# First feed-forward computed by expert in 23 blocks of scattered bf16 rows; second layer entered by halves; third layer's tables loaded earlier

## The chip, the cores and the metric

The kernel is one program on one core of a Trainium2 chip. The metric is the device time of an execution in microseconds, smaller is better. The core's engines are TensorE (PE: matmuls, with PEld its weight loads), VectorE (DVE), ScalarE (ACT), GpSimd (POOL) and SyncE (SP), which here only issues DMAs. The engines run their own instruction streams in order and meet at semaphores. On-chip tensors lie in SBUF; PE writes to eight banks of PSUM, 128 partitions by 512 f32 each.

## The reference

Four layers run over `x` of 2 sequences by 512 tokens by 256 features. Each layer is

```
xn = layernorm(x);  x = x + attention_l(xn) * silu(ffn_l(xn))
```

The change concerns the feed-forward of layer 0, which is computed over all 1024 tokens:

```
shared_out = sigmoid(xn @ shared_gate.T) * (xn @ shared_up.T) @ shared_down.T     # 176 hidden, f32
weights = softmax(xn @ router_w.T)                                                # 8 experts
top_w, top_idx = top_k(weights, 2)
ge, ue = einsum('nh,eih->nei', bf16(xn), bf16(w_gate / w_up))                     # 176 hidden each
de = einsum('nei,ehi->neh', sigmoid(ge) * ue, bf16(w_down))
routed = (bf16(comb)[:, :, None] * de).sum(experts)                               # comb: top_w at top_idx, else 0
return xn + shared_out + routed
```

The layer attention is causal with 16 heads of 16 features in layer 0, plain with 16 query and 4 key heads in layer 1, causal with heads of 128 features in layers 2 and 3. The feed-forward of layer 1 has the same shape as that of layer 0 (8 experts, 2 chosen), but in f32, with silu, a gated shared expert of 352 hidden features and normalised weights.

## The kernel before

Tokens lie in 8 tiles of 128; `B = 2` sequences have `TPB = 4` tiles each. `X` holds the residual, `XN` the normalised rows, `XNT` its transpose, `S` the attention's output. All work is ordered by hand: each engine's program is a list of helpers called layer by layer, and waits on counters between them.

**Start of a layer.** On VectorE `ln_stats` and `ln_scale` each take a half (a sequence); GpSimd computes `rstd` between them (`ln_rstd`). PE turns the rows (`ln_transpose`, L605), ScalarE copies them to `XNT` (`ln_copy`), PE projects (`project01`, L662 and L669 in layer 0, L679 in layer 1). In layer 0 VectorE's `stack_split` makes bf16 parts of queries and keys and PE turns them (L637). In layer 1 GpSimd and VectorE rotate (L488, L489, L1730, L1732), GpSimd computes the RMS factors (L556 to L561), and ScalarE starts the parts with `stack1_first` (L1250). Layer 1 starts after the last row of layer 0's feed-forward; layer 2 is already entered by halves from `shared1`.

**Attention of layers 0 and 1** (`attention01`) runs over `NG = 4` groups of 4 heads and over 8 stages in a group. In layer 0 PE also computes scores for the row maxima of the next group (`max_scores`, L701, L703) in two banks, which VectorE reduces (`row_maxima`, L1765) before PE may write them again. The router's softmax and choice of two experts (`probabilities`, `largest`, L1605 to L1620, and `combine_weights`) run on VectorE in the last group of layer 0.

**Feed-forward of layer 0** (`ffn0`) is dense. In a loop over the two sequences, for 11 tiles of 128 hidden features of all experts, PE computes gate and up (4 bf16 matmuls of 512 columns, L1042) and spreads the combination weights (L1045), ScalarE takes the sigmoid (L1460), and VectorE multiplies twice (L1944, L1947); two tiles of the shared expert are among them. Then for each token tile PE sums 13 matmuls of 256 columns (L1058), and VectorE, ScalarE and VectorE again apply the residual, silu and update (L1961, L1464, L1955, L1957).

**Feed-forward of layer 1.** When its router is done, PE ranks the tokens (`ranks`), VectorE computes a slot for each token and choice (`slots`, 15 operations, L1650 to L1665), and GpSimd scatters the rows of `XN` to `xg` in HBM by 16 indirect DMAs during the attention (`scatter`, in `stage_v`). After the attention, `experts1` runs over `NBLK = 23` blocks of 128 rows, each of one expert. A turn of its loop on PE is

```
turn_rows(i)        # L1073, two transposes
turn_hidden(i - 3)  # L1091, two transposes
owner[i - 1] = pe.value_load(...)   # L1110: the expert's number, from SBUF to a register
gate_up(i - 1)      # L1081, 352 columns, weights' address by the register
down(i - 3)         # L1099, 256 columns, the same
```

with ScalarE at the activation (L1478) and a copy of the turned hidden rows, and VectorE at three operations a block: `store_rows` (L1973), `hidden` (L1979), `store_y` (L1986). SP brings the blocks in fours and writes the results to `yg`. Then PE turns the heads (`turn_heads`, L828) and projects (`out_projection`, L845), while GpSimd gathers each token's two results by 16 more indirect DMAs (`gather`, L524) once the last block is written. `shared1` computes the shared expert (L1132), VectorE multiplies (L2016) and between these sums the gathered rows (`weigh`, L2003, L2004); then come the down matmuls (L1143) and the residual (L2026, L2009, L2010), with the entry of layer 2 in their second half.

**Layer 2's tables.** SP issues `rope2`, `mask_row`, `wa`, `wb` and `bout` after the last down matmul of `shared1` (L401 to L405); VectorE's `attention2` begins with a wait for all five, ahead of its first rotation (L1865).

Of the kernel before, what the change touches and what calls it, by code (L numbers as in the profile page):

```python
# [18 lines left out]
F32 = mybir.dt.float32  # L19
BF16 = mybir.dt.bfloat16  # L20
F16 = mybir.dt.float16
ALU = mybir.AluOpType
# [37 lines left out]
N_CONST = 10  # L60

def build(nc, W, out):
    ctx = ExitStack()
    with ctx:
# [20 lines left out]
        seltab = sb("seltab", [P, E * IE], BF16)  # L86
        sel0 = seltab[0:E, :]
        mask_row = seltab[:, 0:SEQ]
# [13 lines left out]
        combT = sb("combT", [E, TOK], BF16)  # L102
# [63 lines left out]
        NE0 = E * IE  # L166
        w2b = W2[:, :].bitcast(BF16)
        eg0 = w2b[:, 0:DC * NE0].rearrange("p (c n) -> p c n", c=DC)
        eu0 = w2b[:, DC * NE0:2 * DC * NE0].rearrange("p (c n) -> p c n", c=DC)
        ed0 = w2b[:, 2 * DC * NE0:2 * DC * NE0 + 11 * D].rearrange("p (m n) -> p m n", m=11)  # L170
        o = (2 * DC * NE0 + 11 * D) // 2
        sg0 = W2[:, o:o + DC * HS0].rearrange("p (c n) -> p c n", c=DC)
        su0 = W2[:, o + 352:o + 704].rearrange("p (c n) -> p c n", c=DC)
        sd0 = W2[:, o + 704:o + 704 + 2 * D].rearrange("p (m n) -> p m n", m=2)
        I2 = 2 * IE
        HC = IE // 2
        egu1 = W2[:, 0:E * DC * I2].rearrange("p (e c n) -> p e c n", e=E, c=DC)
# [8 lines left out]
        tri_b = W1[:, 800:864].bitcast(BF16)  # L186
        one_b = W1[:, 864:928].bitcast(BF16)
        steps_f = W1[:, 928:992].rearrange("p (e k) -> p e k", e=E)
        upto_f = W1[:, 992:1056].rearrange("p (e k) -> p e k", e=E)
        block_f = W1[:, 1056:1056 + NBLK * E].rearrange("p (n e) -> p n e", e=E)  # L190
# [13 lines left out]
        xb0 = r1b[:, 0:2048].rearrange("p (c t) -> p c t", c=DC)  # L204
        he0 = r1b[:, 2048:2048 + 11 * 512].rearrange("p (m t) -> p m t", m=11)
        hs0 = R1[:, 4096:5120].rearrange("p (m t) -> p m t", m=2)
        act01 = [R1[:, 5120 + 512 * i:5632 + 512 * i] for i in range(2)]
        prod01 = [R1[:, 6144 + 512 * i:6656 + 512 * i] for i in range(2)]
        h1 = R1[:, 7168:7168 + 3 * TOK].rearrange("p (m t) -> p m t", m=3)
        xblk = R2[:, 2048:2048 + 2 * QUAD * D].rearrange("p (r d) -> p r d", d=D)  # L210
        xblkT = [R1[:, 256 * i:256 * i + 256] for i in range(2)]
# [61 lines left out]

        HID0 = [(128 * m, 128) for m in range(11)]
        SH0 = [(0, HS0 // 2), (HS0 // 2, HS0 // 2)]
        SH1 = [(128 * m, min(128, HS1 - 128 * m)) for m in range(3)]

# [1989 lines left out]
```

## Time and profile before

| | us |
|---|---|
| median of 3 runs (lowest, highest) | 1410.25 (1404.46, 1412.22) |
| the profiled execution: its time | 1396.9 |
| its span, first to last instruction | 1395.1 |
| attention of layer 0 ends, heads are turned | 191.4 |
| last row of layer 0's feed-forward | 275.4 |
| layer 1's first `stack1_first` | 296.6 |
| layer 1's blocks | 398.5 to 460.8 |
| layer 2's first rotation | 522.8 |

Positions are from the span's start. PE is busy 90% of the span, so a change moves the time where PE waits, or where PE has less to do and nothing else takes its place. The profiled execution lies 13.3 us below the median of the runs.

### The profile page before, as it was taken

To read this page: it belongs to the slowest core of one execution; us is meant where nothing else is said; L and a number is where in the kernel's file an instruction comes from. 1 tells how busy PE (TensorE), PEld (TensorE's weight loads), DVE (VectorE), ACT (ScalarE), POOL (GpSimd) and SP (SyncE) were. 2 spreads that over 40 slices of the span, in tenths; PEclk is the share of its full clock that TensorE was granted. 3 is DMA by queue.
4 is the path that set the end of the run, shared out by engine and by line. 5 is a ranking of instruction groups with operands and counts; after the bars stand their busy time and mean duration, and the time that the engine had idled before them with its cause. 6 is when DMAs were issued, how large, how long until landed. Compare 5 with 4: busy or idle time off the path is not lost.

```text
span 1395.1 us, 19093 instructions
## 1 busy us (share of the span) xinstructions
PE 1249.1 (90%) x6418; PEld 778.0 (56%) x6418; DVE 743.6 (53%) x2033; ACT 611.6 (44%) x1518; POOL 107.8 (8%) x130
## 2 busy tenths in 40 slices
PE   4888888768999968999999999989999999999994
PEld 3644443344257544556565587656666666666853
DVE  4777625656134258888888740244444434446357
ACT  1634453258952213555555502344444445442053
POOL 3230000052300400000000000000000000000000
PEclk9989999968999988999999999989999999999998
DMA  8000000130212420000000001010000000000000
GB/s 223 12 2 2 2 27 0 54 114 16 77 46 73 147 83 16 12 12 12 13 8 8 5 1 72 9 67 23 12 24 15 20 24 12 24 12 1 1 0 30
DMA packets 25965, 45.75 MB, mean 33 GB/s; under 512 B 3711, under 2 KB 22111, under 8 KB 24551
## 3 DMA queue, kind: packets, MB, share of 16 engines
q1 hardware_dynamic: 23622, 35.25, 7.8%
q0 software_dynamic: 2256, 9.37, 2.3%
q8 instruction: 51, 0.84, 0.2%
q14 instruction: 36, 0.29, 0.1%
HBM read 37.50 MB, written 9.18 MB: 33 GB/s over the span
## 4 chain that ended last, share of the span: by engine, by line
PE 69%; DVE 14%; issue 10%; ACT 4%; DMA 1%; POOL 1%; SPq 1%; ACTq 0%; DVEq 0%; POOLq 0%
PE bank L860 12%; PE bank L876 8%; PE bank L867 8%; PE bank L845 5%; PE bank L853 5%; PE bank L871 4%; PE bank L746 4%; PE bank L730 3%; PE bank L1081 2%; PE bank L1042 2%; DVE W L1765 2%; PE bank L1176 2%; PE bank L1132 1%; PE bank L1099 1%; PE bank L1162 1%
## 5 line engine op out<-in xcount | busy, mean ns | idle before, releaser
L1206 ACT COPY R<-bank 128x512 f32<-128x512 f32 (+4 forms) x203 | 110.5, 560 | 323.4 <-PE bank L876 142.8
L1838 DVE CUSTOM_DVE_ANT_0 bank<-bank,seltab 128x128 f32<-128x128 f32 (+3 forms) x256 | 127.0, 497 | 173.2 <-PE bank L867 170.8
L860 PE MATMUL bank<-XNT,W 128*128 128x512 f32 x416 | 203.3, 613 | 6.8 <-ACT R L1206 3.8
L1343 ACT ACTIVATE R<-bank,nm 128x128 f32<-128x128 f32 (+3 forms) x256 | 136.2, 532 | 109.4 <-DVE nm L1838 108.5
L867 PE MATMUL bank<-R 128*128 128x512 f32 (+3 forms) x384 | 134.3, 434 | 0.0
L860 PEld LDWEIGHTS bank<-XNT,W 128*128 128x128 f32 x416 | 76.4, 194 | 102.8 <-issue 94.7
L1319 ACT ACTIVATE PT<-bank 128x512 f32<-128x512 f32 (+3 forms) x256 | 109.1, 520 | 43.3 <-PE bank L735 40.1
L845 PE MATMUL bank<-W,R 128*128 128x256 f32 x576 | 125.3, 380 | 2.7 <-ACT R L1206 2.7
L845 PEld LDWEIGHTS bank<-W,R 128*128 128x128 f32 x576 | 109.1, 190 | 18.1 <-issue 1.9
L871 PE MATMUL bank<-identf,R 128*128 128x128 f32 x640 | 112.3, 275 | 6.6 <-DVE R L1855 4.9
L876 PE MATMUL bank<-PT,R 128*128 128x128 f32 (+3 forms) x384 | 112.0, 435 | 5.6 <-ACT PT L1206 4.3
L1206 ACT COPY PT<-bank 128x128 f32<-128x128 f32 (+3 forms) x256 | 108.7, 426 | 15.2 <-PE bank L871 15.1
L871 PEld LDWEIGHTS bank<-identf,R 128*128 128x128 f32 x640 | 79.2, 141 | 58.6 <-issue 33.4
L876 PEld LDWEIGHTS bank<-PT,R 128*128 128x128 f32 x384 | 71.2, 190 | 61.4 <-issue 37.8
L853 PEld LDWEIGHTS bank<-W,XNT 128*128 128x128 f32 x640 | 76.5, 192 | 9.5 <-issue 7.6
L853 PE MATMUL bank<-W,XNT 128*128 128x128 f32 x640 | 77.9, 275 | 0.0
L1765 DVE TENSOR_REDUCE W<-bank 128x1 f32<-128x128 f32 (+3 forms) x128 | 57.3, 487 | 26.6 <-PE bank L703 26.6
L730 PE MATMUL bank<-R 96*128 96x512 bf16 (+4 forms) x256 | 66.0, 355 | 5.1 <-DMA R<-W 2.2
L746 PE MATMUL bank<-PT,R 128*32 128x512 f32 (+3 forms) x512 | 59.6, 539 | 0.6 <-ACT PT L1319 0.6
L867 PEld LDWEIGHTS bank<-R 128*128 128x128 f32 x384 | 58.2, 191 | 1.1 <-issue 0.5
L605 PE MATMUL bank<-identf,XN 128*128 128x128 f32 x64 | 15.7, 427 | 44.9 <-DVE XN L1577 44.9
L730 PEld LDWEIGHTS bank<-R 99*128 99x128 bf16 (+1 forms) x256 | 23.1, 100 | 56.3 <-ACT PT L1319 36.3
(258 smaller groups left out, 1819.1 us busy)
## 6 DMA issues: line engine op xcount, KB each, us to landing
W<-in_wq SPq DMA_DIRECT2D x32, 128.0 KB, 2.0
W<-in_wo SPq DMA_DIRECT2D x2, 2048.0 KB, 8.5
W<-in_egu SPq DMA_DIRECT2D x1, 2816.0 KB
W<-in_wk SPq DMA_DIRECT2D x20, 128.0 KB, 2.1
W<-in_wv SPq DMA_DIRECT2D x20, 128.0 KB, 2.0
R<-xg SPq DMA_DIRECT2D x5, 512.0 KB, 4.6
yg<-R SPq DMA_DIRECT2D x5, 512.0 KB, 3.2
W<-in_wa SPq DMA_DIRECT2D x2, 1024.0 KB, 6.4
```

The source lines that it names most:

```text
L730: ins = mm(dst[:, q0:SEQ], kstk[0:rows, g * GH + h if l == 0 else g, b * SEQ + j * P:b * SEQ + (j + 1) * P], qstk[0:rows, g * GH + h, b * ...
L746: ins = mm(PS[OUT_BANK][32 * h:32 * h + 32, q0:SEQ], vs[b][:, j, h if l == 0 else 0, :], PT[:, w % 2, h, q0:SEQ], start=j == 0, stop=j == ...
L845: ins = mm(PS[4 + m % 4][:, 0:D], heads[:, k, m * P:(m + 1) * P], w[:, k, :], start=k == 0, stop=k == n - 1)
L853: ins = mm(bank[:, t * P:(t + 1) * P], XNT[:, c, b * SEQ + t * P:b * SEQ + (t + 1) * P], wqkv23[:, 2, c, :], start=c == 0, stop=c == DC - 1)
L860: ins = mm(bank[:, :], wqkv23[:, s, c, :], XNT[:, c, b * SEQ:(b + 1) * SEQ], start=c == 0, stop=c == DC - 1)
L867: return mm(PS[u % 4][:, 0:n], q[:, t * P:n], k[:, 0:n], start=True, stop=True)
L871: ins = tr(PS[4 + u % 2][:, j * P:(j + 1) * P], Pr[u % 4][:, j * P:(j + 1) * P], identf[:, :])
L876: ins = mm(PS[6][:, j * P:SEQ], v[:, j, :], PT[:, slot, j, j * P:SEQ], start=j == 0, stop=j == TPB - 1)
L1206: return nc.scalar.copy(dst, src)
L1319: fn(PT[:, w % 2, h, q0:SEQ], PS[SCORE_BANK[h]][:, q0:SEQ], ACT.Exp, scale=HD ** -0.5).then_inc(cb["pb_ready"], 1)
L1343: return fn(Pr[c][:, 0:n], PS[c][:, 0:n], ACT.Exp, scale=-1.0, bias=nm[:, c:c + 1], accum_out=esum[:, c:c + 1])
L1838: return dve.tensor_tensor_reduce(out=s[:, 0:n], in0=s[:, 0:n], in1=mask_row[:, SEQ - n:SEQ], scale=-1.0, scalar=-MASKED, op0=ALU.add, op1 ...
```

## The change

Layer 0's feed-forward takes the form of layer 1's. `experts1` and `shared1` become `experts(l)` and `shared(l)`, `ffn0` goes. For layer 0 the rows are cast to bf16 on GpSimd (`xb`) and scattered to an `xg` of their own in groups 2 and 3 of the attention; all matmuls and transposes of its blocks are bf16. The router's work on VectorE moves from the last group into `project01`, the ranks into the start of the attention, the slots into group 1. The routing tables get a place of their own and are loaded at the start, as is `mask_row`. The entry of layer 1 is split by halves, as layer 2's was: the first half is normalised and turned inside `shared(0)`, tiles 0 to 3 are projected, then the second half is turned. Of layer 2's tables, `rope2` and `bout` are issued when layer 1's last gate-up is done, `wa` and `wb` behind the last output projection and ahead of `wo2`. Layer 1's weights are issued after the last residual sum of layer 0.

```diff
@@ SP
-                         (sel0, "sel0"), (rw0, "rw0"),
+                         (mask_row, "mask_row"), (rw0, "rw0"),
+            sp.dma_start(route[:, 0:128].bitcast(BF16), W["route_b"]).then_inc(ld["const"], 16)
+            sp.dma_start(route[:, 128:440], W["route_f"]).then_inc(ld["const"], 16)
...
+            move_blocks(0)
             sp.wait_ge(out_ps, NT)
             sp.dma_start(wqkv1, W["wqkv1"]).then_inc(ld["attn1"], 16)
             sp.dma_start(wo1, W["wo1"]).then_inc(ld["attn1"], 16)
...
-            sp.wait_ge(ffn[0]["y_ps"], NT)
-            sp.wait_ge(zeroed, 32)
+            sp.wait_ge(ffn[0]["f"], NT)
...
+            move_blocks(1)
+            sp.wait_ge(gu_blk, NBLK * 2)
+            sp.dma_start(rope2, W["rope2"]).then_inc(ld["ffn2"], 16)
+            sp.dma_start(bout, W["bout2"]).then_inc(ld["ffn2"], 16)
             sp.wait_ge(out_ps, NT * 2)
-            sp.dma_start(wo23, W["wo2"]).then_inc(ld["wo2"], 16)
-            sp.wait_ge(ffn[1]["y_ps"], NT)
-            sp.dma_start(rope2, W["rope2"]).then_inc(ld["ffn2"], 16)
-            sp.dma_start(mask_row, W["mask_row"]).then_inc(ld["ffn2"], 16)
             sp.dma_start(wa, W["wa2"]).then_inc(ld["ffn2"], 16)
             sp.dma_start(wb, W["wb2"]).then_inc(ld["ffn2"], 16)
-            sp.dma_start(bout, W["bout2"]).then_inc(ld["ffn2"], 16)
+            sp.dma_start(wo23, W["wo2"]).then_inc(ld["wo2"], 16)
@@ GpSimd
+                        if l == 0 and g == 0 and b == 1:
+                            own(pool.tensor_copy(xb, XN[:, :, :]))
+                        scatter(l, SCATTER_AT[l].get(g * B + b, ()))
...
+            pool.dma_start(xg[0].rearrange("(p j) d -> p j d", p=P), zeros_b).then_inc(zeroed, 16)
...
-            pool.wait_ge(coreb[0]["st_ps"], NG * B * GH * TPB)
-            pool.tensor_copy(xb0, XNT[:, :, :]).then_inc(xb_ready, 1)
-            ln_rstd(1)
-            pool.wait_ge(ot_sb, 2)
+            gather(0)
+            pool.wait_ge(ot_sb, LN_PAIRS)
             pool.wait_ge(out_ps, NT)
             pool.memset(R2[:, 0:1024], 1.0).then_inc(const_made, 1)
+            ln_rstd(1)
@@ PE
                 else:
-                    pe.wait_ge(xnt_ready, 2 * LN_PAIRS)
+                    pe.wait_ge(xnt_ready, LN_PAIRS + 2)
                     for m in range(NT):
+                        if m == TPB:
+                            ln_transpose(1, (2, 3))
+                            pe.wait_ge(xnt_ready, 2 * LN_PAIRS)
...
                 if l == 0:
                     stk_copied(0)
                     pe.sem_inc(nm_ps, 2)
+                    ranks(0, PS[0])
...
-                    if l == 1:
-                        experts1()
+                    experts(l)
                     turn_heads(l)
                     out_projection(l, OT01, (wo0, wo1)[l], DC)
-                    if l == 0:
-                        ffn0()
-                    else:
-                        shared1()
+                    shared(l)
@@ ScalarE
-                    for m in range(TPB + 1):
+                    for m in range(TPB):
                         take(m)
+                    ln_copy(1, (2, 3))
+                    take(TPB)
@@ VectorE
                         stack_split(m)
+                        if m == 0:
+                            probabilities(0)
+                        elif m <= 2:
+                            largest(m - 1)
+                        elif m == 3:
+                            chosen(0)
...
-                        if causal and last and w == 0:
-                            probabilities(l)
-                        elif causal and last and w in (1, 2):
-                            largest(w - 1)
-                        elif causal and last and w == 4:
-                            combine_weights()
+                        if causal and g == 1 and w == TPB - 1:
+                            slots()
...
+                    take_ranks(0, PS[0])
...
+                per_gate = NT // (B * nm - 2)
...
+                    if l == 0:
+                        own(stt(out=wx[:, m, :], in0=px[:, 1, m, :], scalar=rs[:, 5, m:m + 1], in1=XN[:, m, :],
+                                op0=ALU.mult, op1=ALU.add))
+                        own(stt(out=wx[:, m, :], in0=px[:, 0, m, :], scalar=rs[:, 4, m:m + 1], in1=wx[:, m, :],
+                                op0=ALU.mult, op1=ALU.add))
...
+                    if 1 <= k < B * nm - 1:
+                        for m in range(per_gate * (k - 1), per_gate * k):
+                            weigh(m)
...
-                ln_stats(2, 1)
+                ln_stats(l + 1, 1)
+                if l == 0:
+                    ln_scale(1, 1)
```

In `shared(0)` the shared expert has two parts of 88 hidden features, so PE's gate-up has 4 steps in place of layer 1's 6 (`nm = 2`), and VectorE weighs tiles 0 to 3 after the second and 4 to 7 after the third (`per_gate = 4`).

## Rows read from the trace of the kernel before

**Rows 1.** The page: engines' totals, and two rows in 40 slices of 34.9 us

```profile
PE 1249.1 (90%) x6418; PEld 778.0 (56%) x6418; DVE 743.6 (53%) x2033; ACT 611.6 (44%) x1518; POOL 107.8 (8%) x130
PEclk9989999968999988999999999989999999999998
```

**Rows 2.** Stretches: length, busy us (x instructions) by engine, granted clock, DMA

```profile
191.40:275.40 84.00, 73.02 (x318) 35.77 (x318) 42.15 (x72) 29.76 (x51) 0.00 (x0) 0.96 0.05 15
275.40:296.60 21.20, 15.89 (x48) 9.91 (x48) 11.73 (x33) 7.95 (x35) 11.43 (x16) 0.76 0.79 259
301.60:325.50 23.90, 15.15 (x133) 14.26 (x134) 18.62 (x50) 15.57 (x31) 13.02 (x23) 0.50 0.00 1
398.50:460.80 62.30, 59.38 (x280) 43.85 (x278) 25.85 (x71) 15.78 (x46) 0.00 (x0) 1.00 0.24 75
```

**Rows 3.** Timeline: PE turns layer 0's heads; ScalarE begins layer 1's parts

```profile
191.44 1.97 PE L828 MATMUL bank<-identf,R 128*128 128x128 f32 x16 [0.81 <-DVE R L1789]
...
296.58 0.93 ACT L1250 ACTIVATE PT<-R,small 128x768 bf16<-128x768 f32 x1 [2.31 <-POOL small L561]
```

**Rows 4.** Groups in 398.5:460.8, layer 1's blocks: busy us, mean ns, idle before

```profile
L1081 PE MATMUL bank<-W,R 128*128 x92 | 31.6, 466 | 1.1 <-DVE R L1973 0.8 <-issue 0.3
...
L1986 DVE COPY R<-bank 128x256 f32<-128x256 f32 x23 | 9.8, 425 | 6.7 <-PE bank L1099 6.7
```

**Rows 5.** PE's sequencer by line, 400.1:401.3 and, last row, 425.8:427.85: duration, first and last start

```profile
L1071 PEldq EVENT_SEMAPHORE  x2: 51/51/51, 400.2 to 401.2; - x2
L1110 PEldq TENSOR_LOAD <-rt x1: 311/311/311, 400.3 to 400.3; - x1
L1081 PEldq FUSED_REGOPS  x2: 46/46/46, 400.9 to 401.1; - x2
...
L1099 PEldq FUSED_REGOPS  x2: 46/53/60, 426.5 to 426.6; - x2
```

**Rows 6.** Timeline, PE: bf16 transposes of layer 0's stack

```profile
37.20 1.99 PE L637 MATMUL bank<-identb,PT 128*96 128x128 bf16 x32 [1.34 <-DVE PT L1685]
```

**Rows 7.** Timeline, layer 1 from its last block to its down matmuls

```profile
460.12 0.42 DVE L1986 COPY R<-bank 128x256 f32<-128x256 f32 x1 [1.48 <-PE bank L1099]
460.80 1.94 PE L828 MATMUL bank<-identf,R 128*128 128x128 f32 x16 [0.72 <-DVE R L1986]
463.87 1.01 POOL L524 DMA_INDIRECT PT<-yg,rt  x1 [80.40 <-DMA yg<-R]
470.58 20.76 PE L1132 MATMUL bank<-XNT,W 128*128 128x512 f32 x48
...
479.38 0.35 DVE L2003 TENSOR_SCALAR PT<-PT,rs 128x256 f32<-128x256 f32 x1 [0.42 <-DMA PT<-yg,rt]
...
482.70 0.95 POOL L524 DMA_INDIRECT PT<-yg,rt  x1 [0.30 <-issue]
...
492.90 8.03 PE L1143 MATMUL bank<-W,R 128*128 128x256 f32 x36 [1.56 <-DVE R L2016]
```

**Rows 8.** Timeline, GpSimd and VectorE at the entries of layers 1 and 2

```profile
288.22 0.83 POOL L488 TENSOR_TENSOR R<-R,rope 128x160 f32<-128x160 f32 x1 [6.82 <-ACT R L1206]
...
294.90 1.64 POOL L561 TENSOR_TENSOR small<-small,mhalf 128x8 f32<-128x8 f32 x1
...
514.76 0.38 DVE L1570 BATCH_NORM_AGGREGATE mv<-stat 128x2 f32<-128x6 f32 x4
...
522.84 0.69 DVE L1865 TENSOR_TENSOR R<-bank,W 128x512 f32<-128x512 f32 x1 [7.70 <-DMA W<-in_bout]
```

**Rows 9.** Timeline, VectorE: in layer 0's projection; layer 1's `slots`, first and last

```profile
43.45 0.69 DVE L1675 TENSOR_TENSOR PT<-bank,PT 128x512 f32<-128x512 f32 x1 [1.17 <-ACT PT L1206]
...
339.27 0.21 DVE L1650 TENSOR_TENSOR rt<-bank,W 128x64 f32<-128x64 f32 x1
...
342.77 0.17 DVE L1665 CAST rt<-W 1x23 int32<-1x23 f32 x1
```

**Rows 10.** Waits in 90:190, layer 0's attention: us in total, times, longest

```profile
PEld bank L701 <- DVE W L1765: 19.5, 39, 1.2
```

More of the change, by code:

```diff
@@ L218, in build, with two @@
-        yg = nc.dram_tensor("yg", (NBLK * P, D), F32, kind="Internal").ap()
+        def two(t, o, n, rows=P):
+            return [t[0:rows, o + n * i:o + n * i + n] for i in range(2)]
+        xb = W2[:, 9216:10240].bitcast(BF16).rearrange("p (m d) -> p m d", m=NT)
+        xblk = (W2[:, 6144:7168].bitcast(BF16).rearrange("p (r d) -> p r d", d=D),
+                R2[:, 2048:2048 + 2 * QUAD * D].rearrange("p (r d) -> p r d", d=D))
+        yblk = (W2[:, 7168:8192].bitcast(BF16).rearrange("p (r d) -> p r d", d=D),
+                R1[:, 2048:2048 + 2 * QUAD * D].rearrange("p (r d) -> p r d", d=D))
@@ L456, in _, with ln_rstd @@
             pool.wait_ge(const_made, 1)
-            def ln_rstd(l):
-                for b in range(B):
+            def ln_rstd(l, halves=range(B)):
+                for b in halves:
                     r = rstd[:, TPB * b:TPB * (b + 1)]
@@ L572, in _ @@
             stage_v(1)
-            gather()
+            gather(1)
             ln_rstd(2)
@@ L601, in ln_transpose @@
                 for k in pairs:
+                    bank = PS[k + 2 if l == 1 and k >= 2 else k]
                     pe.wait_ge(xn_ready, NT * l + 2 * k + 2)
@@ L711, in turn_maxima, with ranks @@
                 ins.then_inc(nm_ps, 1)
+            def ranks(l, bank):
+                dst = bank[:, 0:NT * E].rearrange("p (m e) -> p m e", e=E)
+                pe.wait_ge(comb_ready, l + 1)
+                mm(dst, tri_b, comb[:, :, :], start=True, stop=False)
+                for m in range(NT - 1):
+                    mm(dst[:, m + 1:, :], one_b, comb[:, m:m + 1, :].broadcast_to([P, NT - 1 - m, E]),
+                       start=False, stop=m == NT - 2)
+                for m in range(NT):
+                    ins = mm(bank[:, NT * E:NT * E + E], one_b, comb[:, m, :], start=m == 0, stop=m == NT - 1)
+                ins.then_inc(rank_ps, 1)
             def attention01(l):
@@ L1483, in experts1, with shared @@
                     if 1 <= i <= NBLK:
-                        silu(i - 1)
-            def shared1():
-                f = ffn[1]
-                nm = len(SH1)
+                        gate(i - 1)
+            def shared(l):
+                f, parts = ffn[l], SHARED[l]
+                nm = len(parts)
                 for k in range(B * nm):
-                    r = SH1[k % nm][1]
+                    r = parts[k % nm][1]
                     act.wait_ge(f["gu_ps"], k + 1)
@@ L2163, in _ @@
                     attention01(l)
-                    if l == 0:
-                        ffn0()
-                    else:
-                        experts1()
-                        shared1()
+                    experts(l)
+                    shared(l)
                 else:
```

458 lines of the change are left out of this document (177 added, 281 removed).

## The prediction

> **What bounds the kernel now.** The page first [rows 1]: PE is busy 90% of the span, so the kernel is PE's work plus the places where PE waits for another engine, and the change must be costed along that path. The granted clock shows where PE ran sparse: the slice 279 to 314 has 0.6, and the slices 488 to 558 have 0.8. Then the stretches [rows 2]: the dense feed-forward takes 84.0 us (191.4 to 275.4), with PE busy 73.0. The entry of layer 1 takes 21.2 more until ScalarE's first part at 296.58 [rows 3]. These 105.2 us are what most of the change rewrites. Layer 1's blocks, which do the same arithmetic in f32, take 62.3 us, with PE busy 59.4 and VectorE 25.9: they are the model for the new blocks, and there PE is the bound. Last, the timelines and the sequencer's own rows show what stands behind PE when its matmuls shrink.
>
> **The blocks.** The 23 f32 blocks cost 62.3/25 = 2.5 us a turn; PE's busy time says the same. In bf16 PE does less. A bf16 transpose takes 1.99/32 = 0.062 us for 128 columns [rows 6], so a turn is 4 x 0.062 for the transposes, 2 x 0.17 for 352 columns and 2 x 0.12 for 256: 0.83 us. So PE's array stops being the bound. Two others are left. VectorE has three operations a block, two copies of 0.42 [rows 4] and a product estimated at 0.34 from its fewer columns, 1.2 us. And PE's sequencer must fetch the expert's number and compute two pairs of addresses. At the start of layer 1's blocks, where it runs ahead of the array, a turn that has only the rows' transposes, the fetch and the gate-up goes from 400.2 to 401.2: 1.0 us [rows 5]. A full turn adds three events (each start about 0.1 after the last) and the down matmul's two register operations (426.5, 426.6 and 0.1 to the next), plus what the hidden rows' transposes hold up the fetch, 0.1: 1.6 to 1.8. I take 1.7. Bounds: 1.2, where VectorE stands, and 2.5, as now.
>
> The durations alone say otherwise: 0.31 + 0.16 and ten entries of 0.05 are 1.0 for a full turn, under VectorE's 1.2; it is the starts that give 1.7. The Trainium skill's Perfetto Trace Analysis, section Sequencer-only Instruction, says that the profiler reports only the execute part, and that the wait and the propagation of semaphores are hidden beside it; by that rule, the trace agrees with the starts. By durations the sum below would be 10 us lower.
>
> Twenty of the turns are full: 20 x 1.7 = 34.0. Of the 62.3, 12.7 is filling and draining; scaled by 1.7/2.5 it is 8.7. PE stood idle 0.8 before it turned the heads [rows 3], which the first block fills. The blocks push `turn_heads` back by 34.0 + 8.7 - 0.8 = 42 us.
>
> **From the last block to the down matmuls.** Two paths. PE's: in layer 1 the shared expert begins 9.8 after the heads' turn (460.80 to 470.58) and takes 20.8 for 6 steps [rows 7]; 4 steps take 13.8, and 1.6 passes until the down matmul: 25.2. GpSimd's: the gather starts 3.1 after the heads' turn (463.87), and 16 indirect DMAs take until 482.70 + 0.95: 19.8. Landing I take at 2.5; above it is bounded by 5.7, since the eighth was issued by 473.7 and VectorE still waited until 479.38. Then VectorE weighs tiles 4 to 7, 8 operations near 0.46, 3.7, and only then makes the last product, 0.7 and 0.2 to PE. Sum 3.1 + 19.8 + 2.5 + 3.7 + 0.9 = 30.0. GpSimd's path is longer by 4.8, since bf16 halves the bytes and not the count of DMAs: 30.0 us. In layer 1 it is hidden by the two further steps.
>
> **From the down matmuls to layer 1's parts.** In layer 1 the down matmuls start at 492.90 [rows 7] and the second half's statistics are done at 514.76 + 0.38 [rows 8]: 22.2. GpSimd's `rstd` takes 1.4. It comes ahead of the rotations in GpSimd's program now, so the rotations and RMS factors of the first half, though projected by then, wait for it: in layer 1 today 288.22 to 294.90 + 1.64 [rows 8], 8.3. Sum 31.9, where splitting alone would promise more. Layer 1's parts start 31.9 after the down matmuls.
>
> **Layer 0's attention, earlier.** The router's 22 small operations move into the projection. Slots' fifteen take 339.27 to 342.94, 0.245 each [rows 9], so these are 5.4 us in four portions; VectorE has gaps of 1.1 before L1675 there, another near its copy, and PE's transposes have their input just in time: 0.5 (bounds 0 and 5.4). `ranks(0)` is 16 small matmuls ahead of the first scores, and a copy: 1.2 (0.5 to 2). `slots()` stands in front of VectorE's `row_maxima` in group 1, where PE already waits on VectorE for 19.5 us in 39 waits [rows 10]: of 3.7 us, PE has about one of work in hand, so 2.7 (bounds 1 and 4). Together 4.4. The scatter, 16 DMAs over two groups, ends in the attention, as layer 1's does; uncovered, its end would cost a few us. Casting the rows lies beside it. What is removed from the last group was in VectorE's idle time: 0.
>
> **Sum of layers 0 and 1.** 4.4 + 42 + 30.0 + 31.9 = 108.3 for 105.2: 3.1 us longer.
>
> **Layer 2's tables.** VectorE waits 7.70 for the last table before its first rotation [rows 8], and the second half's normalisation and PE's next projections stand behind it. The tables' last DMA is now issued some 40 us earlier. The whole gap goes, and PE's rows after it follow: -7.7 (0 if one is late). The gathers of layer 1 now share the queues with `wa` and `wb` as well as `wo2`: +0.5 (0 to 2). PE's pause shrinks from 10 us to some 2, and the slices 488 to 558 at 0.8 [rows 1] gain: -1 (0 to -3).
>
> **Sum.** 3.1 - 7.7 + 0.5 - 1.0 = -5.1 us. Against the profiled execution's 1396.9 that is 1391.8; the median of the runs stands 13.3 above it, so the forecast is 1410.25 - 5.1 = 1405.
>
> **Rivals.**
>
> *The sequencer keeps up.* A turn at VectorE's 1.2 us gives 20 x 0.5 = 10 us more: 1395. For it: the durations. Against it: the starts, which show no wait in them.
>
> *The blocks are no faster than f32.* Place: PE's instruction stream in `experts(0)`. If a turn stays at 2.5, through the register's fetch waiting for the transposes before it, it costs 20 x 0.8 = 16 more: 1421, slower. It decides from a turn of 2.3 us, where 5.1 and the 7 of the bound are used up. For it: in f32 the fetch of 427.2 follows its event by 0.26, against 0.13 at the start. Against: PE's busy time explains 2.5 fully.
>
> *The clock falls in the blocks.* In 301.6 to 325.5 PE is busy 63% in short pieces and the clock is 0.50, 1.2 GHz [rows 2]; the new blocks would keep it busy about half. A turn at that level needs 1.7 us of PE, just the sequencer's. What follows is dense, the heads and output projection, 9.8 us: if all of it runs at 1.2 GHz it adds 9.8, of which the 4.8 by which the gather is later hide half, +5: 1410. The Trainium skill's TensorE: Matmul & The Clock Gate, section What's actually happening, says that the throttled state is the default and activity releases it; by that rule, the low clock in sparse stretches agrees with the trace.
>
> *The third layer's wait does not go*, because the earlier tables land late or the second half's rows bind: +7.7, 1413.
>
> **Chances.** A turn of 1.6 to 1.9 with the rest as summed 0.55 (own range 1399 to 1411); sequencer faster 0.17; clock 0.13; blocks slow 0.10; tables 0.05. A measurement of this kernel tells 0.5% from no change, 7 us: faster under 1403, slower over 1417. The sum lies near the first edge, so of the likeliest case 0.25 is faster, 0.28 the same, 0.02 slower; with the rivals faster 0.42, same 0.42, slower 0.16. The range reaches from below the fast sequencer's 1395, since the attention's 4.4 may be near 1 and the clock may gain there too, to the slow bounds of gather and attention: 1389 to 1417.
>
> **What would show it.** Right: starts of L1110 about 1.7 apart in layer 0's blocks; PE idle there for its own issue, VectorE idle between operations; in `shared(0)` VectorE waits for the gathered rows before `weigh(4)`, and PE's first down matmul waits for VectorE; ScalarE's first part waits for GpSimd's RMS factors; the wait on `bout` is gone and the first rotation follows the statistics. One longer PE wait for L1765 in group 1. The number is wrong if a turn is far from 1.7, if the clock stays at 1.2 GHz past the output projection, or if the attention loses more than 8 us.

## The result

The changed kernel is slower: 1420.11 us against 1408.31 (medians of 15 executions each), a ratio of 1.0082 (95% interval 1.0067 to 1.0098), 11.6 us. The forecast was 1405, or 5.1 us faster.

The profiled execution took 1423.3 us. Of its page: span, the last line of busy times that matters here, the granted clock by 40 slices, and the chain's shares.

```profile
span 1421.5 us, 19408 instructions
PE 1250.8 (88%) x6410; PEld 784.4 (55%) x6412; DVE 747.3 (53%) x2096; ACT 611.9 (43%) x1539; POOL 137.8 (10%) x162
...
PEclk9989978866999998999999999999999999999998
...
PE 66%; DVE 16%; issue 11%; ACT 3%; POOL 1%; another core or an unknown queue 1%; DMA 0%; SPq 0%; ACTq 0%; DVEq 0%; POOLq 0%
```

PE's share fell from 90% to 88% [rows 1]. New is "another core or an unknown queue" in the chain. The chain itself shows where (start, us, what); in this program there is no other core:

```profile
173.92 3.44 another core or an unknown queue
...
260.50 5.05 another core or an unknown queue
...
371.99 5.72 another core or an unknown queue
```

The first lies in layer 0's attention while the scatter's indirect DMAs are issued, the second in `shared(0)` while the gather's are, the third in layer 1's attention while its scatter's are. This is ScalarE in `shared(0)` in the timeline (start, duration, what it did, and in brackets how long it was idle and what ended that):

```profile
265.57 0.59 ACT L1443 ACTIVATE R<-bank 88x512 f32<-88x512 f32 x1 [5.07 <-remote]
271.94 0.59 ACT L1443 ACTIVATE R<-bank 88x512 f32<-88x512 f32 x1 [5.78 <-PE bank L1097]
274.13 0.59 ACT L1443 ACTIVATE R<-bank 88x512 f32<-88x512 f32 x1 [1.59 <-remote]
277.01 0.59 ACT L1443 ACTIVATE R<-bank 88x512 f32<-88x512 f32 x1 [2.29 <-PE bank L1097]
```

A step of the shared expert is 8 matmuls, 3.43 us; undisturbed, as below, ScalarE waits 2.84 for it each time. Here the semaphore's counts for the first three steps come 2.0, 5.0 and 3.5 us after the recorded ends of their last matmuls (L1097 at 263.53, 266.96 and 270.61, the counts at 265.55, 271.92 and 274.10). In the profiles without such a wait the count comes within 0.02 us of the end. In the attention one moment holds back two engines. Six matmuls of L703 and L747 end between 174.48 and 175.07 by their records, and VectorE and ScalarE, which wait for them, both start at 177.4:

```profile
177.38 0.89 DVE L1717 TENSOR_REDUCE W<-bank 128x1 f32<-128x512 f32 x2 [3.46 <-remote]
177.48 0.79 ACT L1278 ACTIVATE PT<-bank 128x128 f32<-128x128 f32 x4 [4.16 <-remote]
```

PE's results come late, and all that wait for PE wait. I call these late results. Two limits belong to the name. The end of a matmul is modelled in the trace, so it doesn't show whether the sums or only the counts were late. And the trace lacks some counts of ScalarE, VectorE and GpSimd in the same stretches; but the engines that wait for those start in time, for example VectorE at 272.57 behind ScalarE's end at 272.54 and PE at 273.31 behind VectorE's at 273.25. Only waits for PE are held up.

### The profile page after: what moved, and what is told of

Read it like the earlier page. It is cut to its first block, busy times and chain, and to the rows that moved or that the text cites. A ratio compares the mean times of both kernels' runs of the same rounds, so it can differ in the third digit from the quotient of the medians.

```text
span 1421.5 us, 19408 instructions
## 1 busy us (share of the span) xinstructions
PE 1250.8 (88%) x6410; PEld 784.4 (55%) x6412; DVE 747.3 (53%) x2096; ACT 611.9 (43%) x1539; POOL 137.8 (10%) x162
## 4 chain that ended last, share of the span: by engine, by line
PE 66%; DVE 16%; issue 11%; ACT 3%; POOL 1%; another core or an unknown queue 1%; DMA 0%; SPq 0%; ACTq 0%; DVEq 0%; POOLq 0%
PE bank L856 12%; PE bank L872 8%; PE bank L863 7%; PE bank L841 5%; PE bank L849 5%; PE bank L867 4%; PE bank L758 4%; PE bank L742 3%; PE bank L1045 3%; PE bank L1065 2%; PE bank L1097 2%; PE bank L1108 2%; DVE W L1717 2%; PE bank L1141 1%; PE bank L701 1%
## 5 line engine op out<-in xcount | busy, mean ns | idle before, releaser
L1788 DVE CUSTOM_DVE_ANT_0 bank<-bank,mask_row 128x128 f32<-128x128 f32 (+3 forms) x256 | 127.0, 497 | 173.5 <-PE bank L863 171.1
L856 PE MATMUL bank<-XNT,W 128*128 128x512 f32 x416 | 200.1, 605 | 7.0 <-ACT R L1167 3.8
L742 PE MATMUL bank<-R 96*128 96x512 bf16 (+4 forms) x256 | 69.2, 366 | 10.0 <-ACT PT L1278 5.5
L1805 DVE TENSOR_SCALAR R<-R,erec 128x128 f32<-128x128 f32 (+3 forms) x128 | 50.4, 394 | 5.2
```

The lines of the kernel that those rows point to most:

```text
L742: ins = mm(dst[:, q0:SEQ], kstk[0:rows, g * GH + h if l == 0 else g, b * SEQ + j * P:b * SEQ + (j + 1) * P], qstk[0:rows, g * GH + h, b * ...
L856: ins = mm(bank[:, :], wqkv23[:, s, c, :], XNT[:, c, b * SEQ:(b + 1) * SEQ], start=c == 0, stop=c == DC - 1)
L1788: return dve.tensor_tensor_reduce(out=s[:, 0:n], in0=s[:, 0:n], in1=mask_row[:, SEQ - n:SEQ], scale=-1.0, scalar=-MASKED, op0=ALU.add, op1 ...
```

## The experiments

They ran in five sets, each kernel of a set beside the kernel before on one chip. A ratio is a kernel's time over that of the kernel before in its set, with the 95% interval in brackets; microseconds are worked out from the ratio unless medians are named. The sets differ in something that turned out to matter, so it stands first: in the profiles of sets 1, 2 and 4 results are late near indirect DMAs, in sets 3 and 5 none are. In the changed kernel's profile of the measurement above they are late too. A difference between two kernels that were not in one set is weaker than the intervals say.

| set | kernel before, median us | late results | runs |
|---|---|---|---|
| 1 | 1409.41 | yes | e1 to e4 |
| 2 | 1408.09 | yes | e5 to e8 |
| 3 | 1395.32 | no | e9 to e12 |
| 4 | 1402.14 | yes | e13 to e16 |
| 5 | 1395.91 | no | e17, e18 |

Sets 3 and 4 ran on the chip of the same number, so the chip does not decide it.

**e1, the kernel before again.**

> The kernel before, unchanged. The first profile of it gave 1396.9 us, below all 15 other executions (1404.46 to 1416.46), while that of the changed kernel (1423.3) lies among its own (1415.26 to 1428.26). Theory A: the changed kernel's stalls of 2 to 6 us that no engine or known queue explains, in layer 1's attention (371.99) and while the gather runs, come in most executions of either kernel and the first profile of before missed them: ratio 1.000, and this profile, 5 to 15 us longer, shows such stalls near the indirect DMAs of layer 1. Theory B: they belong to the change: ratio 1.000, and this profile shows none.

Ratio 0.9992 (0.9976 to 1.0009), profiled at 1410.2 us. Theory A holds. ScalarE in layer 1's attention, in the first profile of before and then in this one:

```profile
350.12 4.03 ACT L1319 ACTIVATE PT<-bank 128x512 f32<-128x512 f32 x8 [0.40 <-PE bank L730]
...
358.69 7.47 ACT L1319 ACTIVATE PT<-bank 128x512 f32<-128x512 f32 x15 [0.34 <-PE bank L730]
```

```profile
355.20 1.08 ACT L1319 ACTIVATE PT<-bank 128x512 f32<-128x512 f32 x2 [5.17 <-remote]
356.54 1.33 ACT L1319 ACTIVATE PT<-bank 128x512 f32<-128x512 f32 x2 [0.25 <-PE bank L730]
359.56 4.03 ACT L1319 ACTIVATE PT<-bank 128x512 f32<-128x512 f32 x8 [1.69 <-PE bank L730]
```

The same program, the same 16 scatter DMAs from 342 on, but here a hole of 5.17 us; the last of them starts at 362.6 in the first profile and at 370.4 in this one. In the shared expert (L1132) it is the same story: ScalarE's longest wait for a step is 7.7 us against 3.1. The DMAs themselves also look different: the busy share of the DMA engines in 40 slices from 340 to 366, first profile and then this one.

```profile
DMA  0000005050505150505050505050500505050500
```

```profile
DMA  0000023232332051423230505142300000000000
```

In the first, with 16 scatter DMAs in the window, each one's packets fall together; in the second, with 12, they are spread over more slices. So the profile on which the prediction rested came from an execution of the kind of sets 3 and 5, and the three timed executions shown beside it were, by their times, of the other kind. The 13.3 us between them are of the size of the gap between the sets' medians, 6 to 14 us, and of e5's 10.6.

**e2, only layer 2's tables moved, in the kernel before.**

```diff
@@ names in brackets stand for the DMAs that load them
+            sp.wait_ge(gu_blk, NBLK)
+            (rope2, mask_row, bout)
             sp.wait_ge(out_ps, NT * 2)
+            (wa, wb)
             sp.dma_start(wo23, W["wo2"]).then_inc(ld["wo2"], 16)
-            sp.wait_ge(ffn[1]["y_ps"], NT)
-            (rope2, mask_row, wa, wb, bout)
```

> The kernel before with only layer 2's tables moved as in the change (rope2, mask_row and bout behind the last gate-up of layer 1's blocks, wa and wb at the end of its output projection, wo2 behind them). The prediction's term: -7.7, +0.5 for the gather beside wa and wb: -7.2 us, ratio 0.995, and VectorE's wait on bout is gone. Rival: wa and wb hold up layer 1's gather by several us (the changed kernel's shared expert there took 24.8 us from first gate-up to last against 20.2 before): -3 us, 0.998.

Ratio 0.9943 (0.9926 to 0.996), -8.0 us: the term is right, the rival falls. VectorE's wait on `bout` is gone, and its first rotation (526.80) follows the statistics without a wait.

**e3, e4: no scatter in layer 0; a plain gather there.**

```diff
@@ e3: scatter; the 16 DMAs are left out
+                if l == 0:
+                    return
...
@@ e4: gather, for layer 0 and each half h, from fixed rows
+                    for k in range(2):
+                        pool.dma_start(picked[0][:, k, TPB * h:TPB * h + TPB, :], rows[:, k]).then_inc(picked_in[h], 16)
```

> The changed kernel without the 16 scatter DMAs of layer 0: its blocks work on zeros. Theory S (scatter): each unit of layer 0's attention that holds four scatter DMAs lost 3 to 4.6 us in the profile, so without them it is 8 to 14 us faster than the changed kernel: ratio to the kernel before 0.998 to 1.002. Rival R (ranks, slots, and the clock that falls after them): the scatter is hidden as predicted and the time stays within 2 us of the changed kernel, ratio 1.007 to 1.009.

> The changed kernel with layer 0's gather of 16 indirect DMAs made four plain DMAs that read the same count of bytes from fixed rows, so that the weighed rows are other rows. Theory: GpSimd's path ends 34 us after the heads' turn and PE's about 26 to 29, so this is 4.8 to 8 us faster than the changed kernel: ratio to the kernel before 1.003 to 1.005. Rival: PE's own path is as long (its stalls inside the shared expert come from elsewhere): under 2 us faster, 1.007 or more.

1.0028 (1.0008 to 1.0047) and 1.0034 (1.0015 to 1.0054): 7.7 and 6.8 us less than the changed kernel's 1.0082. In e4's `shared(0)` ScalarE's waits are even again:

```profile
262.38 0.59 ACT L1449 ACTIVATE R<-bank 88x512 f32<-88x512 f32 x1 [3.06 <-PE bank L1103]
...
269.24 0.59 ACT L1449 ACTIVATE R<-bank 88x512 f32<-88x512 f32 x1 [2.84 <-PE bank L1103]
```

**e5, the kernel before without its own indirect DMAs** (no scatter, a plain gather in layer 1).

> The kernel before without its 16 scatter DMAs in layer 1 and with its 16 gather DMAs there made four plain ones from fixed rows (blocks work on zeros, other rows are weighed). Theory A (PE's results come 2 to 6 us late near GpSimd's indirect DMAs, in layer 1 too): the second profile of the kernel before lost about 6 us in the attention and 5 in the shared expert, so this is 8 to 13 us faster than the kernel before, ratio 0.991 to 0.994. Rival: these DMAs are hidden in layer 1 and only layer 0's cost: within 2 us, 0.999 to 1.001.

0.9925 (0.9897 to 0.9953), -10.6 us, with no late result in the profile; its span, 1394.7 us, is that of the first profile of before, 1395.1. So the 32 indirect DMAs of the kernel before cost it 10.6 us in one kind of execution, and in the other next to nothing: without them it takes 1396.5 us (median), with them 1395.3 and 1395.9 in sets 3 and 5.

**e6, both cuts in the changed kernel.**

> Both cuts at once in the changed kernel: no scatter in layer 0 and a plain gather there. The cuts alone gave 7.7 and 6.8 us. If they add up: 14.5 us faster than the changed kernel, 3 us faster than the kernel before, ratio 0.998, near the -5.1 that was forecast, so that the two are the whole of the error. If they share a cause downstream (one hides the other): 8 to 10 us, ratio 1.001 to 1.003.

0.9984 (0.996 to 1.0009), -2.3 us, within the interval of no change. They add up: 13.8 us under the changed kernel's 1.0082, where the cuts alone sum to 14.5. With as many indirect DMAs as before, the changed kernel stands 2.8 us from the forecast.

**e7, the scatter by plain DMAs of the same queue.**

```diff
+                        if l == 0:
+                            pool.dma_start(xg[0][i * P:(i + 1) * P, :], xb[:, m, :]).then_inc(scattered, 16)
+                            continue
```

> The changed kernel with layer 0's 16 indirect scatter DMAs made 16 plain DMAs of the same bytes from the same queue of GpSimd at the same places, to fixed rows. Theory I: what stalls PE is tied to the indirect DMAs (their descriptors made on the fly), so the time falls as without them: 6 to 8 us faster than the changed kernel, ratio 1.002 to 1.004. Rival T: it is the traffic or GpSimd's queue itself: no faster than 2 us, ratio 1.007 or more.

1.0026 (1.0005 to 1.0046): as fast as with no scatter at all (e3). GpSimd's rows for four plain DMAs, and then one of four indirect ones of the changed kernel:

```profile
140.58 2.15 POOL L519 DMA_DIRECT2D xg<-W  x4
```

```profile
139.67 1.10 POOL L518 DMA_INDIRECT xg<-W,rt  x1 [0.17 <-issue]
```

The bytes and the queue are the same, so neither the traffic nor the queue by itself is the cause: the lateness goes with the indirect form. Two things change along with the form and were not tried apart from it. The plain DMAs write 128 rows in a row, not rows at scattered places, and they keep GpSimd for about half as long. The Trainium skill, DMA: Bandwidth & Descriptors, section SWDGE vs HWDGE vs iDMA, says that GpSimd builds the descriptors of all its DMAs in software, direct and indirect. So who builds them does not tell the two forms apart, and in these runs they differ.

**e8, the kernel before with the tables early and layer 1 entered by halves** (dense feed-forward unrolled, `ln_stats(1, 0)` and `ln_scale(1, 0)` inside its second half's products, the rest as in the change).

> The kernel before with the two parts of the change that need no experts: layer 2's tables early and layer 1 entered by halves (dense feed-forward unrolled over its two halves, first half's statistics and normalisation inside the second half's products). Tables: -8.0 as measured. Halves: of the 21.2 us from the last down matmul to ScalarE's first part, the first half's normalisation, transposes and four projections, 5 to 9 us, go under other work: ratio 0.988 to 0.991. Rival: the rotations wait for the second half's rstd on GpSimd anyway and only 2 to 3 us are gained: 0.992 to 0.993.

0.9906 (0.9881 to 0.9932): -13.2 us, of which 5.2 are left for the halves beside the 8.0 that e2 gave to the tables in another set. ScalarE there waited 5.4 us for GpSimd's memset of the stack, behind `rstd` in its order; e12 mends that.

**e9 and e14, half the scatter; e10 and e15, a gather that nothing waits for.**

```diff
@@ e9, e14: the second expert's rows are not scattered
-                    for k in range(2):
+                    for k in range(1 + l):
...
@@ e10, e15: layer 0's rows are weighed from xb, not from the gathered ones; the wait for these moves behind the last statistics
-                        own(stt(out=wx[:, m, :], in0=px[:, 1, m, :], ...
+                        own(stt(out=wx[:, m, :], in0=xb[:, m, :], ...
...
```

> The changed kernel with 8 of layer 0's 16 indirect scatter DMAs, one expert's rows of each token only, two in each of the four units. Theory N (each indirect DMA costs PE its share): 7.7 us over 16 is 0.5 each, so this is 3.9 us faster than the changed kernel, ratio 1.0055. Rival F (a fixed cost for each burst, however long): within 1.5 us of the changed kernel, 1.007 to 1.009.

> The changed kernel with layer 0's 16 indirect gather DMAs issued as before, but VectorE weighs rows that already lie in SBUF and waits for the gather only after the down matmuls. If GpSimd's path alone is the cost, as the prediction has it: as with the plain gather, 6.8 us faster than the changed kernel, 1.0034. If the indirect DMAs hold up PE's own shared expert (its results came 2, 5 and 1 us late there): 2 us faster or less, 1.007. Between them: the shares.

> The changed kernel with 8 of layer 0's 16 indirect scatter DMAs, as before. On a chip with late results: each DMA its share, 3.9 us faster than the changed kernel beside it; rival, a fixed cost for each burst: under 1.5 us faster. On a chip without: no more than 1 us between them.

> The changed kernel with layer 0's gather issued but not waited for by VectorE's weighing, as before. On a chip with late results: faster than the changed kernel by GpSimd's path alone, 2 to 5 us; the rest of the 6.8 of the plain gather is PE's late results. On a chip without them GpSimd's path is all that the gather costs: the prediction's 4.8 us faster.

Without late results, e9 0.9989 (0.997 to 1.0009) and e10 0.9992 (0.9974 to 1.001): nothing gained against the whole kernel's 0.9987 (e17), so neither that half of the scatter nor GpSimd's gather is on the path there. The 4.8 us that the prediction gave to GpSimd's longer path are not there. With them, e15 is 1.0089 (1.0073 to 1.0106), 0.8 us under the changed kernel of its set by the medians: little of the 6.8 us of e4 is a wait for rows, so what the gather costs is in the main PE's late results. e14 is 1.0046 (1.0024 to 1.0068), 7.6 us under it by the ratios and 9.5 by the medians, more than either theory allowed. Its executions spread from 1400.7 to 1416.8. In its profiled one, the fastest, nothing in layer 0's attention waits for a late result, while `shared(0)` has them: ScalarE starts on its second step at 258.88, 3.2 us behind the end of the step's matmuls at 255.69. So a set with late results can hold executions that are free of them in one stretch, and the cost is neither a share for each DMA nor a fixed price for a burst. How it grows stays open.

**e11, the second half's rstd behind two rotations.**

> The changed kernel with GpSimd's rstd of layer 1's second half issued behind its first two rotations instead of ahead of all. The prediction's step: the rotations wait for this rstd, and with it ScalarE's first part, 8.3 us in all: without the wait 2 to 4 us faster, ratio 1.005 to 1.007. Rival: VectorE's own normalisation of the second half stands ahead of its rotations in its order, so GpSimd's third rotation starts no earlier: 0 to 1 us, 1.0075 to 1.008.

0.999 (0.9973 to 1.0006), in a set without late results, against 0.9987 for the kernel without the edit in set 5: nothing, as the rival has it. GpSimd's third rotation in e11, which waits for VectorE:

```profile
293.35 0.64 POOL L490 TENSOR_TENSOR R<-R,rope 128x160 f32<-128x160 f32 x1 [2.56 <-DVE R L1680]
```

**e12 and e16, the best of it, from the kernel before.** The edit is that of e8 and, beyond it:

```diff
-            ln_rstd(1)
             pool.wait_ge(ot_sb, 2)
             pool.wait_ge(out_ps, NT)
             pool.memset(R2[:, 0:1024], 1.0).then_inc(const_made, 1)
+            ln_rstd(1, (0,))
...
                 rotate_sin(m)
+                if m == 1:
+                    ln_rstd(1, (1,))
```

> The kernel before with layer 2's tables early and layer 1 entered by halves (1395.3 us, ratio 0.9906), and GpSimd's order mended: the memset of the stack ahead of the rstd, for which ScalarE waited until 284.4 though the first projection was done by 279.4, and the second rstd behind two rotations. If ScalarE's take of the first tiles binds: 3 to 4 us faster than without, ratio 0.988. Rival: the second half's normalisation binds: under 1.5 us, 0.990.

> The kernel before with layer 2's tables early, layer 1 entered by halves and GpSimd's order mended, as before (ratio 0.9884 there). It adds no indirect DMA, so the ratio should be the same on a chip with late results: 0.985 to 0.990; rival: its denser second half of layer 0 loses there, 0.991 or more.

0.9884 (0.9855 to 0.9912) and 0.989 (0.9872 to 0.9908): 16.2 us faster than the kernel before in set 3, without late results, and 15.4 in set 4, with them. This is the version that beats both, and it keeps the dense feed-forward. It also shows what the change's large part does where no result is late. The changed kernel has the early tables and the entry by halves too and gains only 1.8 us (e17), where these two give the dense kernel 13 to 16 (e8, e12). By this difference, between kernels of different sets, the feed-forward by expert itself costs 11 to 14 us even where no result is late.

**e13 and e17, the changed kernel again.**

> The changed kernel, unchanged, beside the kernel before on one chip. In the last four profiles, all of one chip, no matmul's result came late near an indirect DMA, the kernel before took 1395.3 us there (1408 to 1409 on the chips of the first eight), and cuts of the indirect DMAs in layer 0 left the time where an uncut variant had it (0.999, 0.999, 0.999). Theory C (the chip decides): with late results in this profile the ratio is 1.007 to 1.010, without them 0.997 to 1.001. Theory E (the variants of those runs were faster for their own edits): 1.007 to 1.010 with or without.

> The changed kernel once more beside the kernel before. Three of four sets of runs had profiles with PE's results late near indirect DMAs (the kernel before at 1402 to 1409, the changed one at ratio 1.008 and 1.010), one had none (the kernel before at 1395, three variants of the changed one at 0.999), and the last set ran on the chip of the one without, so that it is no property of the chip. Theory: with late results in this profile 1.007 to 1.011, without 0.997 to 1.001.

e13, with late results: 1.01 (1.0082 to 1.0117), +14.0 us. e17, without: 0.9987 (0.9967 to 1.0007), -1.8 us, within the interval of no change. Theory C holds for the late results, though it is not the chip. Nor do they look random: two profiles of the changed kernel, from different sets of runs, agree in them. The long waits for PE in layer 0's attention are 4.16 and 2.10 us for ScalarE and 3.46 and 2.12 for VectorE in e13's profile, and 4.16 and 2.07, 3.46 and 2.13 in the changed kernel's first one, at the same instructions. ScalarE in `shared(0)` of e13 and of e17:

```profile
268.78 0.59 ACT L1443 ACTIVATE R<-bank 88x512 f32<-88x512 f32 x1 [5.08 <-remote]
273.08 0.59 ACT L1443 ACTIVATE R<-bank 88x512 f32<-88x512 f32 x1 [3.71 <-remote]
```

```profile
258.95 0.59 ACT L1443 ACTIVATE R<-bank 88x512 f32<-88x512 f32 x1 [2.84 <-PE bank L1097]
262.38 0.59 ACT L1443 ACTIVATE R<-bank 88x512 f32<-88x512 f32 x1 [2.84 <-PE bank L1097]
```

**e18, the slots in the last group** (`g == 3` for `g == 1`, and no scatter in layer 0).

> The changed kernel without layer 0's scatter (as in the third experiment, ratio 1.0028 beside the kernel before) and with its slots computed in the last group of its attention instead of the second. Slots' price in the second group was set at 2.7 us; the traces without indirect DMAs in layer 0 show 3.5 us in its unit and 1.5 in the next. In the last group VectorE has no maxima to make. If the traces are right: 4 to 5 us faster than without the scatter alone, 9 to 13 faster than the changed kernel. Rival: the last group is as tight: within 1.5 us of the kernel without the scatter alone, 7 to 9 faster than the changed kernel.

0.9964 (0.9946 to 0.9982), 3.2 us under e17 by the ratios and 3.6 by the medians of the same set. If the scatter is free there, as half of it was in e9, the slots' chain costs 3.2 to 3.6 us more in group 1 than in the last group. The two intervals overlap, so the prediction's 2.7 is not excluded.

## Why the prediction was wrong

It failed at two steps that belong together, the scatter's and gather's cost and the offset of 13.3 us. *"The scatter, 16 DMAs over two groups, ends in the attention, as layer 1's does; uncovered, its end would cost a few us"* was costed at 0, and the gather only as a path of its own on GpSimd. Neither asks what an indirect DMA does to PE. And *"the median of the runs stands 13.3 above it"* was carried over as a constant. Most of it was the price of the 32 indirect DMAs that the kernel had (10.6 by e5), and the change makes them 64. In that kind of execution the change is 11.6 to 14.0 us slower. Without layer 0's 32 it is 2.3 faster (e6), so these cost 13.8 where the prediction has 0 for the scatter and 4.8 for GpSimd's path. Where no result is late the change is 1.8 faster (e17), which these runs do not tell from no change.

The profile after lies 26.4 us above the profile before, 1423.3 to 1396.9, where the timed executions differ by 11.6: the two profiled executions were of different kinds. e17's profile is the one to read against [rows 1 to 10]. By the prediction's own terms:

*The blocks.* PE's fetches of the expert's number in e17 (count, durations in ns, first and last start):

```profile
L1076 PEldq TENSOR_LOAD <-rt x23: 297/300/706, 195.3 to 232.9; - x23
```

37.6 us for 22 turns, 1.71 each: 1.7 was right. So was its reason, the sequencer's starts rather than its durations [rows 5], and e13 shows it best, where the clock was at its upper level, 2.4 GHz, for most of the blocks (first row: length, busy us by engine, granted clock; second row: as above):

```profile
214.30:244.80 30.50, 18.74 (x140) 11.61 (x139) 15.08 (x53) 12.40 (x37) 0.00 (x0) 1.00 0.22 62
L1076 PEldq TENSOR_LOAD <-rt x17: 297/302/706, 215.0 to 242.8; - x17
```

There 16 turns take 27.8 us, 1.74 each, with the array busy 61% and VectorE 49%: neither is the bound. The rivals of a fast sequencer and of slow blocks fall. In e17 the mean granted clock from 196 to 238.5 was 0.70, made of stretches at 1.2 and at 2.4 GHz. From 216.6 to 226.6, at 1.2 GHz, PE is busy 9.1 of 10.0 us and five turns (217.5 to 226.4) still take 1.8 each, so there the array fills the sequencer's 1.7, as the third rival worked out. Then the heads and the output projection took 13.4 us against 9.8 in layer 1 [rows 7]: that rival's mechanism is there, with 3.6 us. PE turned the heads at 238.43, 47.0 after before's 191.44, where 42 + 4.4 were forecast. The last transposes of the attention, ahead of both, split this:

```profile
189.98 0.66 PE L758 MATMUL bank<-identf,R 128*128 128x128 f32 x4 [0.81 <-DVE R L1807]
```

```profile
194.99 0.66 PE L770 MATMUL bank<-identf,R 128*128 128x128 f32 x4 [0.82 <-DVE R L1759]
```

The first is from before, the second from e17: the attention ends 5.0 later, for 4.4 forecast, and the blocks push the heads back by 42.0, as forecast. In e10 and e11, with the same attention, it ends at 192.6 and 192.0, so these 5.0 are one profile's and others have 2.0 and 2.6.

*The attention.* GpSimd's copies of the values mark the units of layer 0's attention, in e17 and in the changed kernel's first profile:

```profile
140.38 0.61 POOL L503 COPY R<-R 128x512 f32<-128x512 f32 x1 [16.85 <-DVE R L1741]
154.54 0.61 POOL L503 COPY R<-R 128x512 f32<-128x512 f32 x1 [8.43 <-DVE R L1741]
168.41 0.61 POOL L503 COPY R<-R 128x512 f32<-128x512 f32 x1 [8.31 <-DVE R L1741]
180.67 0.61 POOL L503 COPY R<-R 128x512 f32<-128x512 f32 x1 [6.70 <-DVE R L1741]
```

```profile
138.88 0.61 POOL L503 COPY R<-R 128x512 f32<-128x512 f32 x1 [16.85 <-DVE R L1741]
153.74 0.61 POOL L503 COPY R<-R 128x512 f32<-128x512 f32 x1 [9.12 <-DVE R L1741]
170.51 0.61 POOL L503 COPY R<-R 128x512 f32<-128x512 f32 x1 [11.21 <-DVE R L1741]
187.54 0.61 POOL L503 COPY R<-R 128x512 f32<-128x512 f32 x1 [11.45 <-DVE R L1741]
```

Four scatter DMAs follow each copy. From copy to copy the units last 14.2, 13.9 and 12.3 us in the first and 14.9, 16.8 and 17.0 in the second, 8.4 us more in three units; the last unit, up to the last transposes, adds 3.3 (17.6 for 14.3). e3 gives 7.7 for the scatter over many executions. Without late results the last copy comes 7.7 later than before (172.93 there) and the attention's end only 5.0 later. The last unit is 2.7 shorter than before, 14.3 for 17.1. It lies in the group that the router's work has left, and the prediction put what is removed there at 0. So 4.4 came near as the sum of a loss that was put too low and a gain that was left out; that the router's work is the whole of the gain was not tried.

*Heads' turn to the down matmuls.* 30.0 forecast. PE's timeline in e17:

```profile
238.43 3.65 PE L828 MATMUL bank<-identf,R 128*128 128x128 f32 x16 [0.71 <-DVE W L1903]
242.75 9.30 PE L841 MATMUL bank<-W,R 128*128 128x256 f32 x32 [0.68 <-ACT R L1167]
251.88 13.90 PE L1097 MATMUL bank<-XNT,W 128*88 128x512 f32 x32
269.93 5.29 PE L1108 MATMUL bank<-W,R 88*128 88x256 f32 x14 [4.15 <-DVE R L1940]
```

31.5 from 238.43 to 269.93, and the place is right (PE waits for VectorE's last product, L1940). The mechanism is not. VectorE did not wait for gathered rows:

```profile
259.58 0.68 DVE L1940 TENSOR_TENSOR R<-R,bank 88x512 f32<-88x512 f32 x1 [2.75 <-ACT R L1443]
260.18 0.47 DVE L1922 SCALAR_TENSOR_TENSOR W<-PT,rs,XN 128x256 f32<-128x256 bf16 x1
...
264.34 0.68 DVE L1940 TENSOR_TENSOR R<-R,bank 88x512 f32<-88x512 f32 x1
264.94 0.47 DVE L1922 SCALAR_TENSOR_TENSOR W<-PT,rs,XN 128x256 f32<-128x256 bf16 x1
...
269.10 0.68 DVE L1940 TENSOR_TENSOR R<-R,bank 88x512 f32<-88x512 f32 x1
```

It weighs tiles 0 to 3 and, behind the third product, tiles 4 to 7 without a pause, 16 operations at 0.52 us each, and starts with the first only after the second product, since the list puts `weigh` behind steps 1 and 2 of 4. The 25.2 of PE's path left this work and the 3.6 of the clock out, and GpSimd's path counted half of the work. That the sum came near was luck.

*Down matmuls to layer 1's parts.* 31.9 forecast; 269.93 to ScalarE's first part at 302.86 is 32.9. The order on GpSimd is as read (`rstd` at 292.71, rotations from 294.03, RMS factors until 302.8), but e11 shows that VectorE's order stands behind it as well.

*Sum of layers 0 and 1.* +3.1 forecast, 302.86 for 296.58 is +6.3 in e17's profile. The 3.2 between them are 0.6 in the attention, 0.0 in the blocks, 1.5 from the heads to the down matmuls and 1.0 behind these.

*Layer 2's tables.* -7.7 with +0.5 for contention, -8.0 in e2: right. In e17 the first rotation follows the statistics with no wait:

```profile
522.41 0.38 DVE L1513 BATCH_NORM_AGGREGATE mv<-stat 128x2 f32<-128x6 f32 x4
522.71 0.66 DVE L1815 TENSOR_TENSOR R<-bank,W 128x512 f32<-128x512 f32 x1
```

So where no result is late the forecast of -5.1 missed the measured -1.8 by 3.3 us, about what these sizes explain in one profile; -5.1 lies a little outside e17's interval, -4.6 to +1.0. The rest of the miss of 16.7 us (-5.1 forecast, +11.6 measured) is the price of the indirect DMAs.

**Open.** What makes results late, and why in three sets of five, was not found. Shown is that they come only near indirect DMAs (e5 has none, e3 and e4 have none in the stretches that they clear), not near plain ones of the same queue (e7), and that the chip's number does not decide it. Not tried is whether an indirect DMA to consecutive rows does it too, or a plain one to scattered rows. That the packets of such DMAs then lie spread out (e1) goes with it; which is cause was not tried.

## What to carry to other kernels

If the profiled execution lies well outside the timed ones, as here by 13.3 us where the timed ones spread by 8, the profile misses a cost; find its place before adding to what causes it, and take a second profile. That the landing of an indirect DMA is hidden does not make it free: count them, and where PE is the bound measure the same kernel without them or with plain ones. Of a change with several parts, price each alone. Here the two cheap ones (tables early, entry by halves) were worth 13 to 16 us, and the large one took most of it back even where no result was late.

## What was not expected of the hardware

Near GpSimd's indirect DMAs, the semaphore counts of matmuls came 1 to 5.6 us after the recorded ends of the matmuls (the longest in e3's `shared(0)`, 252.50 to 258.10). This was so in whole sets of runs and not in others, for the same program: 1395 and 1396 against 1402 to 1409 us. Waits for the other engines' work were not held up. One indirect DMA of 128 rows holds GpSimd 0.95 to 1.2 us and the next mostly starts 0.30 later, in f32 and bf16 alike; a plain one of the same bytes as the bf16 one holds it 0.54.
